# Fourteen of 98 target tiles summed from gathered rows, the other 84 swept in blocks of twelve

## The reference

```python
out_deg = segment_sum(ones, src); in_deg = segment_sum(ones, dst)
src_norm = clip(out_deg, 1) ** -0.5; dst_norm = clip(in_deg, 1) ** -0.5
feat0 = relu(layernorm(x))
def step(f, _):                       # ten times
    f = f * src_norm[:, None]
    agg = segment_sum(f[src], dst)    # 200,000 edges, 32 features
    f = agg * dst_norm[:, None]
    f = (1 - 0.1) * f + 0.1 * feat0
x = x + scan(step, feat0)
```

## Time and profile before

| | |
|---|---|
| median of three runs | 6998.82 us |
| the profiled execution: its span (no other time of it is given) | 7018.8 us |
| TensorE matmuls busy | 5576.3 us (79%) |
| VectorE busy | 4279.1 us (61%) |
| GpSimd busy | 1693.3 us (24%), none after 2993 us |
| first matmul of the sweep, at | 3003.25 us |
| one step of propagation | 398.1 us |

### The profile page before, as it was taken

One profiled execution on the slowest core, in us unless ns is written; L12 is line 12 of the kernel. 1 busy time (PEld: TensorE's weight loads), 2 busy tenths in 40 slices (PEclk: granted clock), 3 DMA queues, 4 the chain that ended last, 5 costly groups with the idle time before them and its releaser, 6 DMA issues. The chain is left out here.

```text
span 7018.8 us, 211605 instructions
## 1 busy us (share of the span) xinstructions
PE 5576.3 (79%) x85008; PEld 3590.0 (51%) x85008; DVE 4279.1 (61%) x12668; ACT 721.3 (10%) x1695; POOL 1693.3 (24%) x1739
## 2 busy tenths in 40 slices
PE   1455555555555556589999999999999999999998
PEld 1344444444444445446565554656555565656564
DVE  7455555555555557766666666666656666666665
ACT  0122222222222223000000000000000000000000
POOL 5655555555555552500000000000000000000000
PEclk9867676666667767799999999999999999999999
DMA  4322222222222222155545555555555555555554
GB/s 117 77 75 76 76 76 77 75 76 77 79 72 79 72 76 94 27 205 194 200 183 204 192 198 205 189 200 191 201 191 201 191 201 201 189 203 189 197 197 169
DMA packets 442864, 1016.61 MB, mean 145 GB/s; under 512 B 253162, under 2 KB 371914, under 8 KB 387354
## 3 DMA queue, kind: packets, MB, share of 16 engines
q1 hardware_dynamic: 386938, 968.76, 39.0%
q0 software_dynamic: 54944, 33.96, 2.6%
HBM read 838.78 MB, written 176.58 MB: 145 GB/s over the span
## 5 line engine op out<-in xcount | busy, mean ns | idle before, releaser
L1864 PE MATMUL banks_fast<-count_units_fast,feature_parts_fast 128*32 128x512 fp8e3 x70608 | 3826.3, 379 | 31.6 <-DVE count_units_fast L1759 26.9
L1864 PEld LDWEIGHTS banks_fast<-count_units_fast,feature_parts_fast 128*32 128x32 bf16 x70608 | 2146.2, 97 | 1688.5 <-issue 37.5
L1758 DVE TENSOR_SCALAR count_units_fast<-packed_ring_fast 128x512 int32<-128x512 int32 x2949 | 1255.8, 426 | 1429.1 <-PE banks_fast L1864 1398.2
L144 POOL DMA_INDIRECT rows_fast<-row_table,idx_fast x1456 | 1408.5, 967 | 996.9 <-ACT count_stage_fast L1257 563.4
L1759 DVE TENSOR_SCALAR count_units_fast<-packed_ring_fast 128x512 int32<-128x512 int32 x2949 | 1237.2, 420 | 0.0
L1351 PE MATMUL banks_fast<-w1a_b1a_fast,turn_fast 49*128 49x96 f32 x3136 | 374.6, 375 | 810.6 <-ACT turn_fast L1262 589.6
L1223 DVE TENSOR_SCALAR window_place_hot_fast<-iota_wide_fast,local_keys_fast,target_weight_fast 128x196 bf16<-128x196 f16 x3136 | 933.9, 343 | 0.0
L1316 PE MATMUL banks_fast<-window_place_hot_fast,window_src_hot_fast 128*128 128x196 bf16 x3136 | 697.4, 312 | 115.4 <-issue 71.0
L1322 PE MATMUL banks_fast<-window_place_hot_fast,window_src_hot_fast 128*128 128x196 bf16 x3136 | 680.2, 305 | 106.1 <-issue 105.4
L1351 PEld LDWEIGHTS banks_fast<-w1a_b1a_fast,turn_fast 49*128 49x128 f32 x3136 | 294.9, 260 | 917.4 <-issue 497.4
L1316 PEld LDWEIGHTS banks_fast<-window_place_hot_fast,window_src_hot_fast 128*128 128x128 bf16 x3136 | 410.1, 155 | 224.2 <-issue 148.3
(11 more groups left out here) (282 smaller groups left out, 1551.5 us busy)
## 6 DMA issues: line engine op xcount, KB each, us to landing
packed_ring_fast<-edge_counts SPq DMA_DIRECT2D x422, 1792.0 KB, 7.0
edge_counts<-count_stage_fast SPq DMA_DIRECT2D x100, 784.0 KB
running_sums<-run_sums_fast SPq DMA_DIRECT2D x100, 768.0 KB
rows_fast<-row_table,idx_fast POOLq DMA_INDIRECT x1456
rows_fast<-attrs_padded SPq DMA_DIRECT2D x98, 128.0 KB
attrs_padded<-in_edge_attr SPq DMA_DIRECT2D x1, 12500.0 KB
rows_fast<-row_table,src_ends_fast POOLq DMA_INDIRECT x112
row_table<-h_nodes_fast SPq DMA_DIRECT2D x1, 1568.0 KB, 5.2
```

What stands on the lines that cost most here:

```text
L144: pool.indirect_dma_start(out=self.rows[:, r, c, 0:DN], out_offset=None, in_=b.dram.table, in_offset=bass.IndirectOffsetOnAxis(ap=idx[:, c ...
L1758: nc.vector.tensor_scalar(to[..., 0:P // 8], of, NIBBLES, None, ALU.bitwise_and)
L1864: last = nc.tensor.matmul(b.banks[at:at + DN, SWEEP[m % 2], 0:COLS], parts[:, side, j, k * DN:(k + 1) * DN], of_strip.bitcast(FP8), start= ...
```

## The change

The ten steps treat the target tiles in two ways. Tiles 14 to 97 are swept as before, but in seven blocks of twelve tiles (`TILES` = 12, 384 columns for each matmul, 384 elements for each opening instruction, 1344 KB for each load). The head of two tiles is gone.

Tiles 0 to 13 (`GT` = 14) are summed edge by edge. The edges are sorted by target, so those of one target tile lie in a row. Each lane takes 18 (`GC`) edges of it in a row, and so a tile has 18 lists of 128 edges. For each list GpSimd gathers the 128 source rows (96 bfloat16 values, 192 bytes) by one indirect DMA from a table of the features in the device's memory, and one matmul adds them up: the weights are a one-hot of 128 edges by 128 targets, kept in SBUF for all steps, and the moving part is the gathered rows with 96 columns. ScalarE's queue stores each block's new features into the table of the next step. The new features of listed tiles are made four tiles at a time. The input gets a second form of the edge ends, `in_ends`, with source and target beside each other. A tile with more than 2304 edges sends the kernel to its general way.

```diff
-TILES = 16
-HEAD = J % TILES
-BLOCKS = J // TILES
+TILES = 12
+BLOCKS = (J - GT) // TILES
+LIST_SLOTS = 4
+LISTS_IN_BANK = 4
+        LIST_AT = {(58 + 22 * i) // BLOCK_UNITS * BLOCK_UNITS + max(AHEAD, (58 + 22 * i) % BLOCK_UNITS): i for i in range(GT - 1)}
...
         @block.gpsimd
         def _(pool):
+            for i in range(GT):
+                pool.indirect_dma_start(out=ends[:, i, :, :].rearrange("p c k -> p (c k)"), out_offset=None,
+                                        in_=ins["ends"].rearrange("e (k a) -> (e k) a", a=1),
+                                        in_offset=bass.IndirectOffsetOnAxis(ap=listed_at[:, i:i + 1], axis=0)).then_inc(ends_in, 16)
+            pool.wait_ge(listed, 1)
+            with pool.Fori(0, steps2) as tt:
+                for side in range(2):
+                    pool.wait_ge(table_stored[side], tt * (STEP_STORES * 16) + (STEP_STORES if side else 1) * 16)
+                    for i in range(GT):
+                        n = side * GT + i
+                        pool.wait_ge(rows_used, tt * (2 * GT) + (n + 1))
+                        for c in range(GC):
+                            pool.indirect_dma_start(out=rows[:, n % LIST_SLOTS, c, :], out_offset=None, in_=b.dram.features[side],
+                                                    in_offset=bass.IndirectOffsetOnAxis(ap=idx[:, i * GC + c:i * GC + c + 1], axis=0)) \
+                                .then_inc(rows_in[n % LIST_SLOTS], 16)
...
         @block.scalar
+                        nc.scalar.copy(drain[:, n % 2, :], b.banks[:, SWEEP[n % 2], 0:COLS]).then_inc(drained, 1)
+                        act.wait_ge(fresh, tt * (2 * BLOCKS) + (BLOCKS + n + 1))
+                        store_rows(1 - side, of_block(m))
...
         @block.vector
+            for i in range(GT):
+                nc.vector.tensor_tensor(list_hot[:, i, :, :], b.iota16[:, :].unsqueeze(1).broadcast_to([P, GC, P]),
+                                        local[:, i, :].unsqueeze(2).broadcast_to([P, GC, P]), ALU.is_equal).then_inc(hot_made, 1)
...
         @block.tensor
-            def sweep_head(t, side):
-                        last = nc.tensor.matmul(b.banks[at:at + DN, HEAD_SWEEP, 0:HEAD * P], parts[:, side, j, k * DN:(k + 1) * DN],
-                                                head[:, j // KC, :, j % KC, :].bitcast(FP8), start=(term < STRIPS),
+            def sum_list(tt, side, i):
+                pe.wait_ge(rows_in[n % LIST_SLOTS], tt * (2 * GT // LIST_SLOTS * GC * 16) + (n // LIST_SLOTS + 1) * (GC * 16))
+                for c in range(GC):
+                    last = nc.tensor.matmul(b.banks[:, LIST[k], at * WF:(at + 1) * WF], list_hot[:, i, c, :].bitcast(FP8),
+                                            rows[:, n % LIST_SLOTS, c, :], start=(c == 0), stop=(c == GC - 1))
+                last.then_inc(rows_used, 1)
...
+            pe.wait_ge(hot_made, GT)
             with nc.Fori(0, steps2, engines=[pe.engine], hint_back_edge=True) as tt:
```

More of the change, by code:

```diff
@@ L87, in __init__ @@
         self.counts = dram("edge_counts", (CHUNKS, P, J + SLOTS, KC, P // 2), U8)
+        self.features = [dram(f"feature_rows{side}", (NP, WF), BF16) for side in range(2)]
 class Kept:
@@ L1014, in _ @@
             last.then_inc(summed, 1)
+            nc.tensor.matmul(b.banks[:, 3, 0:GT], ones[0:1, :], start[0:1, 0:GT], start=True, stop=True).then_inc(summed, 1)
 def messages_and_counts(nc, b, edges, same, window_row, tail, out_int, ahead):
@@ L1714, in _ @@
+            with sp.Fori(0, steps2) as tt:
+                for n in range(2 * STEP_CHUNKS):
+                    sp.wait_ge(opened, tt * (2 * STEP_UNITS) + (n + 1) * UNITS)
+                    sp.sem_inc(passed, 1)
+                    load(n)
+            for n in range(RING):
+                sp.wait_ge(opened, STEPS * STEP_UNITS + (n + 1) * UNITS)
+                load(n)
             for slot in range(RING):
-                sp.wait_ge(chunk_in[slot], (STEPS * pairs * (PAIR_CHUNKS // RING) + 1) * 16)
+                sp.wait_ge(chunk_in[slot], (STEPS * STEP_CHUNKS // RING + 1) * 16)
@@ L1787, in step @@
                     ins_.then_inc(chain, 1)
-                    dve.wait_ge(chain, q * CHAIN + steps[0])
-                step(nc.vector.tensor_tensor(t1, per_node(got), spread(gain), ALU.mult))
-                dve.sem_inc(head_read if of_head else folds_read, 1)
+                    dve.wait_ge(chain, before + steps[0])
+                if of_list:
+                    step(nc.vector.tensor_reduce(t2, got, AX.X, ALU.add))
+                    dve.sem_inc(list_read, 1)
+                    step(nc.vector.tensor_tensor(t1, t2, spread(gains), ALU.mult))
+                else:
+                    step(nc.vector.tensor_tensor(t1, per_node(got), spread(gains), ALU.mult))
+                    dve.sem_inc(folds_read, 1)
                 step(nc.vector.scalar_tensor_tensor(out=f, in0=h, scalar=ALPHA, in1=t1, op0=ALU.mult, op1=ALU.add))
-                step(nc.vector.tensor_tensor(t1, f, spread(b.src_norm), ALU.mult))
+                step(nc.vector.tensor_tensor(t1, f, spread(b.src_norm[:, where]), ALU.mult))
                 for k in range(SPLITS):
@@ new lines, in _ @@
+                        first = AHEAD
+                        for at in sorted(at for at in LIST_AT if at // BLOCK_UNITS == m):
+                            sweep_units(tt, n, first, at % BLOCK_UNITS)
+                            first = at % BLOCK_UNITS
+                            sum_list(tt, side, LIST_AT[at])
+                        sweep_units(tt, n, first, BLOCK_UNITS)
+                        sweep_units(tt, n + 1, 0, AHEAD)
+                        fold(tt, n)
+                    sum_list(tt, side, GT - 1)
@@ L2005 @@
         ins[name] = nc.dram_tensor(f"in_{name}", a.shape, mybir.dt.from_np(a.dtype), kind="ExternalInput").ap()
+    pairs = np.full((E + LISTED, 2), PAD_NODE, np.int32)
+    pairs[0:E, 0], pairs[0:E, 1] = inputs["src"], inputs["dst"]
+    arrays["in_ends"] = pairs
+    ins["ends"] = nc.dram_tensor("in_ends", pairs.shape, I32, kind="ExternalInput").ap()
     out = nc.dram_tensor("out_nodes", (N, DN), FP32, kind="ExternalOutput").ap()
```

288 lines of the change are left out of this document (153 added, 135 removed).

## The result

The changed kernel takes 10141.6 us (median of four runs, 10134.6 to 10157.9) against 7000.7 us for the kernel before, run beside it (four runs, 6998.5 to 7004.3). The ratio is 1.4478, with a 95% interval of 1.4459 to 1.4497. The forecast was 6670 us, its range 6600 to 6960. The profiled execution has a span of 10137.5 us.

What follows compares the result with a forecast made beforehand. TensorE was taken to bound the ten steps: 337.5 + 5.0 + 15.1 + 2 = 359.6 us against 398.1. From 7018.8 us, 385 off and 56 on gave 6690 profiled, 6670 as median; range 6600 to 6960.

Steps and rivals of the forecast that it cites:

- GpSimd is hidden with 8 us to spare: Ten steps: the last listed tile's rows land by 351 us, against TensorE's step of 359.6 us.
- GpSimd's pitch of 1.31 us: Gathers in the steps start 1.31 us apart (1.25 to 1.72); TensorE waits from a pitch of 1.35 on.
- Rival (4), instruction supply: Sweep: instruction rate a third above the old sweep's, half the head's surplus, costs a few us; no chance given.
- the sizes on TensorE: Each step: sweep 337.5 us at 41.0 ns a matmul, lists 15.1 at 60 ns, folds 5.0, switching 2.
- VectorE and the gather: Steps: opening instruction 360 ns, VectorE hidden at 288 of 360 us; gathers' mean near 1.0 us, 1.31 apart.
- the start: Before the first matmul: edge ends, indices and 14 one-hots of 2.56 us make TensorE 50 us late, range 30 to 60.
- the range: Forecast's own range 6600 to 6760 us: matmul -1, +41; lists -45, +96; start -20, +10.
- (1): GpSimd becomes the steps' bound: 6784 us at a pitch of 1.40, 6994 at 1.485; chance 0.29 between 6760 and 6985.
- (2): Slower: opening instructions hold each gather at both ends, TensorE waits for rows; pitch 1.72, 7585 us; chance 0.14.

Runs made afterwards that it cites:

- The added gathers: Kernel before, plus 2520 unread gathers by GpSimd in the ten steps, tied to no other engine: 10433.4 us (one run).
- the streams: Three kernels computing nothing of the reference, running instruction streams beside GpSimd gathers, transfers or fills, gather spacing varied; TensorE 24.7 matmuls a microsecond free, 0.7 beside back-to-back gathers.
- the version with fills for two tiles: Changed kernel with two listed tiles instead of fourteen, blocks of sixteen tiles, a GpSimd fill of 384 elements behind each gather: 6925.5 us, ratio 0.9908 to the kernel before.
- with fourteen tiles (384 elements, 252 fills a step): Changed kernel, whole, with a GpSimd fill of 384 elements and a wait for it behind each gather of the ten steps: 8861.2 us (one run).

## Why the prediction was wrong

- **Failed: "GpSimd is hidden with 8 us to spare".** The step asked whether GpSimd would be ready in time, and what VectorE does to a gather. It never asked what a gather does to the others, and so neither the sum nor any rival had a term for it. The added gathers showed it: each of 2520 costs TensorE 1.30 us, some 3260 us in all, and without them the kernel takes 6953 us. The forecast called GpSimd's pitch of 1.31 us a danger only if it grew; it was the shortness of the pitch that hurt.
- **The trace of before had shown it.** TensorE stood tens of microseconds for "issue" on each of several lines of the message layer. Here is one place, beside gathers 1.25 us apart, where matmuls go over to starts 0.7 us apart:

```profile
1505.75 0.25 PE L1316 MATMUL banks_fast<-window_place_hot_fast,window_src_hot_fast 128*128 128x196 bf16 x1
1506.54 0.24 PE L1316 MATMUL banks_fast<-window_place_hot_fast,window_src_hot_fast 128*128 128x196 bf16 x1 [0.55 <-issue]
1507.28 0.24 PE L1322 MATMUL banks_fast<-window_place_hot_fast,window_src_hot_fast 128*128 128x196 bf16 x1 [0.40 <-issue]
1507.99 0.43 PE L1333 MATMUL banks_fast<-identity_fast,rows_fast 128*128 128x128 f32 x2 [0.47 <-issue]
```

- **Rival (4), instruction supply, "a few us": undersized.** It is 19.6 us a step beside the loads; with the 0.8 ns on each matmul that go with the loads too, it is 26 us a step, 260 in all. Even without the stall the kernel would have gained some 1.5% only.
- **Right: the sizes on TensorE.** Without gathers and loads the sweep took 41.2 ns (41.0 forecast), lists 52 ns (60, 131.2 / 2502), folds 6.5 us a step (5.0, line 1908: 65.5 us in ten). The sum 339.5 + 13.1 + 6.5 is 359 us a step, 359.6 forecast.
- **Right: VectorE and the gather.** Opening took 363 ns (360 forecast), a gather 0.96 us (near 1.0) and they started 1.25 us apart (1.31).
- **Right: the start.** A one-hot took 2.54 us (2.56 forecast), and TensorE waited 40.8 us for them, 50 forecast in all.
- **A slip in the range.** The parts that it names (+41, +96, +10) add to 147 and an upper end of 6817 us, not 6760. It changes nothing: both lie far below the measured time, and inside the range of the forecast, which went up to 6960.
- **Rivals (1) and (2)** had GpSimd as the bound. It wasn't: TensorE never waited for rows in a step, and GpSimd waited 2881 us for TensorE. (2)'s sign was right for another reason, which is luck.
- The Trainium skill (SBUF — State Buffer, "SBUF: two separate sides") says of SBUF's ports that a DMA and a compute instruction can't slow each other, and that TensorE never waits on anyone. For plain transfers the streams agree (24.7 matmuls in a microsecond beside them). Beside indirect gathers less than 1.75 us apart TensorE does wait (0.7 matmuls); whether that happens at SBUF's ports no run shows.

**Left open.** What it is in a gather that stalls the engines. The streams exclude fetching, DMA traffic, the bytes, the number of rows and GpSimd being busy. The stall outlasts the last gather by 3 to 22 us, as if each took 1.40 us, so it isn't only that a running gather is held back. That gathers pile up work on a path that all engines need fits these numbers, but it is argued and not shown; nor do they tell why even spacing needs 1.75 us and not 1.40.

## What to carry to other kernels

A free engine is not a free resource: before work is moved to an idle engine, look in the trace for what the others do beside that kind of instruction, above all for "issue" idle time that nothing explains. In the streams here, indirect gathers wanted at least 1.75 us from start to start beside TensorE; back to back, a burst of them cost nearly its whole length on each of the three engines that were tried. When a sweep is made faster, its supply of instructions beside the loads has to be checked too.

## What the runs showed of the hardware

- Back-to-back indirect gathers (pitch 1.25 us) cut TensorE from 24.7 to 0.7 matmuls in a microsecond, ScalarE from 9.8 to 2.3 copies, VectorE from 13.6 to 1.7. Single instructions then start 0.7 us or a multiple apart. The same at 16 rows (0.6 matmuls), 32 bytes, and in a loop of 40 matmuls.
- The stall lasts 3.4 us beyond a burst of 18 gathers and 13.1 beyond one of 84 (21.9 with 16 rows each): in all 1.40 us for each gather.
- VectorE's opening instruction of 512 elements took 446 ns in the mean in the version with fills for two tiles, against 426 before and 426 without the fills; with fourteen tiles (384 elements, 252 fills a step) 410 and 444 ns against 363 and 357.
- A fill of 384 elements took 0.47 us on GpSimd in the mean with fourteen tiles, 0.55 with two and 0.43 in the streams; the wait against a register's value and the count behind it took 0.8 us.
- TensorE's gaps over 0.5 us in the sweep without gathers ended 1.2 to 1.8 us after a 16 KB packet of its instruction queue, all 143 of them.
